# Long filters of a decoder layer: filter taps arranged by channel on GpSimd before TensorE reads them

## The reference, cut to what matters

```python
def fir(x, filt):                       # depthwise, causal, one filter per channel
    y = _dwconv_causal(x.reshape(b, Ll, H * DV), filt.reshape(H * DV, -1))
    return y.reshape(b, Ll, H, DV)
short, long_, wide = fir(v, fir_s), fir(v, fir_l), fir(v, fir_wd)   # 3, 31 and 64 taps
# the statistics of short, long_, wide, delta_out and v feed a gate, and
o = w_ctx[..., 0:1] * short + w_ctx[..., 1:2] * long_ + w_ctx[..., 2:3] * wide + w_ctx[..., 3:4] * delta_out + w_val * v
```

## Time and profile before

| | |
|---|---|
| three executions | 627.75, 627.02, 619.87 us; median 627.02 |
| the profiled execution | 627.85 us, of it span of the engines 626.1 us |
| mean granted TensorE clock | 0.956 of 2.4 GHz |
| HBM | 34.31 MB read, 2.10 MB written |

### The profile page before, as it was taken

The page is one execution under the profiler, slowest core; times in us unless marked ns, Lnnn a source line. Parts: engine busy times, 40 slices in busy tenths (PEclk is TensorE's granted clock), DMA queues, the critical chain, the costliest instruction groups (busy, mean ns, idle before and its releaser), DMA issues. The chain is left out here.

```text
span 626.1 us, 16517 instructions
## 1 busy us (share of the span) xinstructions
PE 540.1 (86%) x7254; PEld 409.9 (65%) x7254; DVE 444.3 (71%) x866; ACT 263.7 (42%) x478; POOL 117.5 (19%) x102
## 2 busy tenths in 40 slices
PE   4776879998999899988799889649999997998993
PEld 1454666767766766776564355538887876887883
DVE  1987758786787778785385999982445668768774
ACT  2675554452444245333237535322333243454441
POOL 1000550061006102601002220270810000010000
PEclk9899879999999999998799999788999998999997
DMA  6700630151014101312134100350000000000001
GB/s 191 237 3 0 199 107 3 37 170 37 4 56 156 33 4 58 115 36 84 56 136 136 34 17 18 113 181 33 1 1 0 2 1 1 0 2 35 9 25 68
DMA packets 26534, 37.47 MB, mean 60 GB/s; under 512 B 4641, under 2 KB 13602, under 8 KB 26463
## 3 DMA queue, kind: packets, MB, share of 16 engines
q1 hardware_dynamic: 26463, 36.42, 18.1%
HBM read 34.31 MB, written 2.10 MB: 58 GB/s over the span
## 5 line engine op out<-in xcount | busy, mean ns | idle before, releaser
L309 DVE SCALAR_TENSOR_TENSOR arena<-bank,conv_w,arena 128x511 f32<-128x511 f32 (+2 forms) x72 | 53.1, 746 | 17.5 <-ACT arena L468 14.2
L1534 POOL COPY arena<-v_win 128x256 f32<-128x256 f32 x32 | 20.3, 662 | 171.2 <-PE bank L786 171.1
L2068 ACT COPY arena<-bank 128x512 f32<-128x512 f32 x40 | 23.3, 585 | 56.4 <-PE bank L1818 37.3
L1818 PE MATMUL bank<-v_win,arena 128*128 128x256 f32 x192 | 46.1, 390 | 0.0
L1201 ACT COPY arena<-bank 128x512 f32<-128x512 f32 x40 | 21.7, 590 | 47.1 <-PE bank L912 47.0
L1818 PEld LDWEIGHTS bank<-v_win,arena 128*128 128x128 f32 x192 | 37.4, 196 | 5.7 <-issue 0.4
L786 PE MATMUL bank<-arena 128*32 128x128 f32 x512 | 35.7, 409 | 4.8 <-ACT arena L1151 3.1
L1800 PE MATMUL bank<-v_win,arena 128*128 128x256 f32 x128 | 32.2, 412 | 7.4 <-DVE arena L2353 4.3
L1156 ACT COPY arena<-bank 128x256 f32<-128x256 f32 x32 | 19.4, 606 | 44.5 <-PE bank L803 44.5
L1800 PEld LDWEIGHTS bank<-v_win,arena 128*128 128x128 f32 x128 | 26.5, 209 | 12.1 <-issue 4.5
L701 PE MATMUL bank<-arena 128*128 128x512 f32 x64 | 32.2, 624 | 0.9 <-PEq L704 0.9
(11 more groups left out here) (286 smaller groups left out, 1372.1 us busy)
## 6 DMA issues: line engine op xcount, KB each, us to landing
arena<-in_toep_w SPq DMA_DIRECT2D x32, 256.0 KB, 3.0
arena<-in_toep_l SPq DMA_DIRECT2D x32, 256.0 KB, 3.8
arena<-in_xT SPq DMA_DIRECT2D x12, 512.0 KB, 4.4
arena<-in_x SPq DMA_DIRECT2D x4, 512.0 KB, 4.2
arena<-in_ctx SPq DMA_DIRECT2D x4, 512.0 KB, 4.3
out<-arena SPq DMA_DIRECT2D x4, 512.0 KB, 2.9
qkv_w<-in_qkv_wT SPq DMA_DIRECT2D x1, 768.0 KB, 5.4
v_win<-in_w_gateT SPq DMA_DIRECT2D x1, 768.0 KB, 4.6
```

The source lines that it names most:

```text
L309: return nc.vector.scalar_tensor_tensor(out=acc[:, j:L], in0=src[:, 0:L - j], scalar=conv_w[:, m, CONV_K - 1 - j:CONV_K - j], in1=acc[:, j:L],
L1534: g.tensor_copy(A2["v_piece"][:, n % 2, :, :].rearrange("p c (t two) -> p t two c", two=2), v_win[:, :, :, n * PIECE:(n + 1) * PIECE].rear ...
L1818: i = mm(oo, src[:, k, f * P:(f + 1) * P], w[:, k, :], start=(k == 0), stop=(k == KT - 1 and f > 0))
L2068: nc.scalar.copy(dst(i), bank[RING_FIRST + n % RING].rearrange("p (t c) -> p t c", c=dst(i).shape[-1]))\
```

## The change

- **Arranging.** From piece 8 (`OPENING`) on, POOL copies each loaded piece from (f, c) to (c, f) order (`arrange`: 128 x 1024 words, read 8 words apart, written side by side), and the moving operand of L786 becomes 128 neighbouring words. `filter_piece(n)` waits for the new semaphore `arranged` instead of the DMA. Pieces 0 to 7 are moved as before.
- **Places.** `TOEP_BUFS` is 5: four places in the arena and one that takes the room of the three biases. The opening uses all five for raw pieces. Afterwards places 0 and 1 are raw, and 3, 4, 2 hold arranged pieces in turn; `arrange(n)` waits until piece n - 3 is done, the load of piece n until piece n - 2 is arranged.
- **POOL's order.** Three pieces are arranged before recurrence 0; then each `copy_piece(n)` is mostly followed by `arrange(n + 1)`, before and after `k_root` and behind `v_scale`.
- **SP's order.** The loads of raw pieces are gated by `arranged`, and the gate weights and the x of block 3 by the last two arrangements.
- **Biases.** Their loads leave block 1 and come in block 3, after a memset by POOL (768 words) at its start; two memsets leave block 1 (`PADS` 15 to 13).

```diff
-TOEP_BUFS = 4
+TOEP_BUFS = 5
+OPENING = 8
-PADS = 15
+PADS = 13
-        xq_b = sb("xq_b", [P, D])
-        xkv_b = sb("xkv_b", [P, 2 * D])
-        xo_b = sb("xo_b", [P, D])
+        late_rows = sb("late_rows", [P, 4 * D])
+        xq_b, xkv_b, xo_b = late_rows[:, 0:D], late_rows[:, D:3 * D], late_rows[:, 3 * D:4 * D]
...
+        raw_slot = lambda n: n % TOEP_BUFS if n < OPENING else n % 2
+        by_channel = lambda n: toep[(3, 4, 2)[(n - OPENING) % 3]].rearrange("p f c -> p (f c)").rearrange("p (c f) -> p c f", c=PIECE)
+        arranged_to = lambda n: n + 1 - OPENING
...
-                load(xq_b[0:1, :], dr["xq_b"].rearrange("(a n) -> a n", a=1))
-                load(xkv_b[0:1, :], dr["xkv_b"].rearrange("(a n) -> a n", a=1))
-                load(xo_b[:], dr["xo_b"].partition_broadcast(P))
...
+                def toep_from(first, last):
+                    for n in range(first, min(last, NPIECE - 1) + 1):
+                        if n < OPENING + 2:
+                            sp.wait_ge(s2["fir_mm"].sem, n - TOEP_BUFS + 1 if n < OPENING else n - 2)
+                        else:
+                            sp.wait_ge(s2["arranged"].sem, arranged_to(n - 2))
+                        load_toep(sp, n)
...
-                    pe.wait_ge(toep_in[n % TOEP_BUFS], 32 * (n // TOEP_BUFS + 1))
+                    if n < OPENING:
+                        pe.wait_ge(toep_in[raw_slot(n)], 32 * times_loaded(n))
+                        taps = toep[raw_slot(n)].rearrange("p f c -> p c f")
+                    else:
+                        pe.wait_ge(s2["arranged"].sem, arranged_to(n))
+                        taps = by_channel(n)
...
-                               A2["v_piece"][:, n % 2, c, :], toep[n % TOEP_BUFS][:, :, c], start=True, stop=True)
+                               A2["v_piece"][:, n % 2, c, :], taps[:, c, :], start=True, stop=True)
...
+                def arrange(n):
+                    pool.wait_ge(toep_in[raw_slot(n)], 32 * times_loaded(n))
+                    pool.wait_ge(s2["fir_mm"].sem, (4, 5, 8)[n - OPENING] if n < OPENING + 3 else n - 2)
+                    g.tensor_copy(by_channel(n), toep[raw_slot(n)].rearrange("p f c -> p c f")).then_inc(s2["arranged"].sem, 1)
...
+                arrange(OPENING)
                 copy_piece(OPENING)
+                arrange(OPENING + 1)
                 copy_piece(OPENING + 1)
+                arrange(OPENING + 2)
...
+                    copy_and_arrange(piece[2], piece[2])
+                    copy_piece(piece[3])
+                    k_root(b + 1)
+                    arrange(piece[4])
+                    copy_and_arrange(piece[4], piece[-1] - 1)
+                    copy_piece(piece[-1])
+                    q_roots(b + 1)
+                    v_scale(b + 1)
+                    arrange(piece[-1] + 1)
+                    copy_and_arrange(piece[-1] + 1, FIRST_OF[b + 1] + 1)
...
+                g.memset(late_rows[:, 0:3 * D], 0.0).then_inc(s4["sentinels"].sem, 1)
```

More of the change, by code:

```diff
@@ L265, in layer @@
         TOEP = 2 * DK * PIECE
-        toep = [arena[:, WL + i * TOEP:WL + (i + 1) * TOEP].rearrange("p (f c) -> p f c", c=PIECE) for i in range(TOEP_BUFS)]
+        toep = [arena[:, WL + i * TOEP:WL + (i + 1) * TOEP] for i in range(TOEP_BUFS - 1)] + [late_rows[:, :]]
+        toep = [x.rearrange("p (f c) -> p f c", c=PIECE) for x in toep]
         A2 = carve(arena, {
@@ L288, in load_keys_xT @@
             sp.dma_start(A2["xT"], dr["xT"][b].rearrange("(k p) t -> p k t", p=P)).then_inc(s2["xT_in"].sem, 16)
+        raw_slot = lambda n: n % TOEP_BUFS if n < OPENING else n % 2
+        times_loaded = lambda n: sum(raw_slot(k) == raw_slot(n) for k in range(n + 1))
+        by_channel = lambda n: toep[(3, 4, 2)[(n - OPENING) % 3]].rearrange("p f c -> p (f c)").rearrange("p (c f) -> p c f", c=PIECE)
+        arranged_to = lambda n: n + 1 - OPENING
         def load_toep(sp, piece):
-            i = piece % TOEP_BUFS
+            i = raw_slot(piece)
             for f in range(2):
@@ L706, in _ @@
             def _(sp):
[L708 to L715, removed]
+                def toep_from(first, last):
[5 more added lines that the diff above has]
+                        load_toep(sp, n)
+                toep_from(TOEP_BUFS, OPENING - 1)
                 sp.wait_ge(s2["beta_mm"].sem, 1)
                 load_keys_xT(sp, 1)
[L718 to L729, removed]
+                at = OPENING
+                for b in range(B - 2):
+                    toep_from(at, FIRST_OF[b] + 4)
+                    at = FIRST_OF[b] + 5
+                    sp.wait_ge(s2["beta_mm"].sem, s2["beta_mm"].at(b + 1, 1))
+                    load_keys_xT(sp, b + 2)
+                toep_from(at, NPIECE - 1)
+                sp.wait_ge(s2["arranged"].sem, arranged_to(NPIECE - 2))
                 sp.dma_start(g1x_w, dr["g1x_wT"].rearrange("(k p) n -> p k n", p=P)).then_inc(g1x_in.sem, 16)
-                sp.wait_ge(s2["fir_mm"].sem, NPIECE - TOEP_BUFS + 2)
+                sp.wait_ge(s2["arranged"].sem, arranged_to(NPIECE - 1))
                 load_turned_rows(sp, 0)
@@ L1566, in _, with copy_and_arrange @@
                 v_scale(0)
+                arrange(OPENING)
                 copy_piece(OPENING)
+                arrange(OPENING + 1)
                 copy_piece(OPENING + 1)
+                arrange(OPENING + 2)
+                def copy_and_arrange(first, last):
+                    for n in range(first, last + 1):
+                        copy_piece(n)
+                        if n + 1 < NPIECE:
+                            arrange(n + 1)
                 for b in range(B):
                     piece = pieces_of(b)
[L1571 to L1581, removed]
+                    if b == B - 1:
+                        copy_piece(piece[2])
+                        continue
+                    copy_and_arrange(piece[2], piece[2])
[8 more added lines that the diff above has]
+                    copy_and_arrange(piece[-1] + 1, FIRST_OF[b + 1] + 1)
         def of_batch(b):
@@ L1693, in _ @@
                 load_rows(sp, 1)
+                sp.wait_ge(s4["sentinels"].sem, 1)
+                sp.dma_start(xq_b[0:1, :], dr["xq_b"].rearrange("(a n) -> a n", a=1)).then_inc(dc_loaded.sem, 16)
+                sp.dma_start(xkv_b[0:1, :], dr["xkv_b"].rearrange("(a n) -> a n", a=1)).then_inc(dc_loaded.sem, 16)
+                sp.dma_start(xo_b, dr["xo_b"].partition_broadcast(P)).then_inc(dc_loaded.sem, 16)
                 for b in range(2, B):
```

15 lines of the change are left out of this document (7 added, 8 removed).

## The result

The changed kernel takes 620.22 us (median of 20 executions, 615.91 to 625.92), the kernel before, on the same chip, 625.64 us (median of 20, 618.35 to 629.49). The ratio is 0.9934 with a 95% interval of 0.9912 to 0.9957: 0.7% less, 0.4 to 0.9% by the interval, and so within 2% of no change. A ratio leaves out the slower executions of a kernel (over 1.5% above its fastest) and a median keeps them, so a ratio can differ from that of the medians: here the ratio means 4.1 us and the medians 5.4 us. The forecast of 629 us had the wrong sign.

A forecast was written before the change was run, and what follows sets the result against it. In the recurrences PE (busy 86%) and DVE were taken as two halves of a chain, DVE's waits limiting the gain. -0.8 + 1.75 + 1.75 + 1.3 - 2.2 = +1.8 us, 628.8 against the median, said as 629; range 617 to 637.

The forecast's parts named there:

- step 4: Recurrence 0: arrange(13), 135.3 to 137.7 us, holds L1338, which ends at 139.3 instead of 138.15: +0.6 us.
- step 6: End of recurrence 0: arrange(14) and arrange(15) fall on both L1354; the second ends at 152.6 instead of 150.85: +1.75 us.
- the signs named beforehand: Trace observations listed as showing the forecast right: L786 at 0.64 us, a POOL copy of 2.3 to 2.6 us, held DVE lines.
- The matmuls, 0.64 us: Pieces 8 to 31 on PE: 1.11 us falls to 0.64; undisturbed -1.2 us each in recurrences 0 and 1, -0.7 in 2.
- The rival of matmuls that do not get shorter: PE's pieces: four matmuls side by side, not the stride, make 1.11 us; gains vanish, holds stay: 634 us, chance 0.05.
- The arrangement, 2.4 us: POOL's strided copy of 1024 words, 24 times: 2.4 us each, with 0.97 and 2.6 us carried as ends.
- Step 1: Start of recurrence 0: arrange(11), 126.4 to 128.8 us, holds L1324, which ends at about 128.85 instead of 128.35: +0.5 us.
- Batch 3, -2.2: Pieces 25 to 31: 25 gains nothing, the others 0.47 or 0.27 us each; -2.2 us, bounds 0 and -3.3.
- Biases, -0.8: Block 1: bias loads leave the queue before batch 2's x, which comes 1.05 us earlier: -0.8 us, bounds -1.05 and 0.
- POOL late: Rival at piece 12: an arrangement of 2.8 us or more makes POOL late; at 4 us, 640 us in all; chance 0.09.
- Short holds: Rival: an arrangement near 1 us, or one that lets DVE through, gives -6.1 us, 621 us; chance 0.25.
- Clock and stalls: Rival: more PE idle time could bring the low clock into a recurrence, 4 us either way; chance 0.11, half each side.

The follow-up runs named there:

- the host's order: Kernel before with biases moved and the host laying out pieces by channel from piece 8, nothing arranged: 619.77 us, ratio 0.9871; run again 617.09 us, 0.9867.
- the two repeats: The changed kernel, unaltered, timed twice more beside later experiments against the kernel before: 619.51 us, ratio 0.9888, and 620.7 us, ratio 0.9852.
- arrangements behind the masks: Changed kernel, but POOL waits after v_scale until DVE has finished both L1357 before arranging the next recurrence's first piece: 620.28 us, ratio 0.992.

## Why the prediction was wrong

In short: the mechanism was right, and its price was too high. For recurrences 0 to 2 the forecast set 7.9 us of holds against 3.1 us of gain. Compared at like clocks the arrangements cost 3.6 us there, and the shorter matmuls give 4.1 to 4.5 us. The terms that failed are step 4, +0.6 us where about nothing was held, and step 6, 1.65 us where 0.55 was; both go back in part to the arrangement, taken at 2.4 us where it is 2.07. Of the signs named beforehand, PE's pieces at 0.64 us, the x of batch 2 earlier by 1 us or more, and no wait of PE for an arrangement came; a copy of 2.3 to 2.6 us, L1324 over 0.9, L1338 over 2 us for two and L1354 over 1.5 us did not.

**The matmuls, 0.64 us: right, its yield in the recurrences too low.** Recurrence 0 with neighbouring words and no arranging is 58.12 us in all three profiles, 1.57 us under before; I gave 1.2. In recurrence 2 it is 30.05 us, 1.1 us less; I gave 0.7. The limit "only what the small waits around DVE allow" was too tight by 0.4 us each. The rival of matmuls that do not get shorter is out.

**The arrangement, 2.4 us: too high, it is 2.07.** I took the value near the upper bound because its strides looked like those of `copy_piece`. This size decided more than itself, since steps 4 and 6 asked whether a copy runs into an instruction.

**Step 1, L1324 held: the hold is there, but it falls on L1317.** DVE, changed kernel:

```profile
122.34 1.21 DVE L1309 TENSOR_TENSOR arena<-arena 128x1024 f32<-128x1024 f32 x1
...
124.93 1.09 DVE L1320 TENSOR_SCALAR arena<-arena 128x16 f32<-128x16 f32 x1
125.94 0.66 DVE L1322 TENSOR_SCALAR arena<-arena 128x16 f32<-128x16 f32 x1
...
126.92 0.17 DVE L1327 TENSOR_TENSOR arena<-arena 128x16 f32<-128x16 f32 x1
```

and POOL beside it:

```profile
123.90 2.09 POOL L1544 COPY arena<-arena 128x1024 f32<-128x1024 f32 x1
125.91 0.66 POOL L1537 COPY arena<-v_win 128x256 f32<-128x256 f32 x1
```

L1320, 16 words with one input, ends at 126.02, with the arrangement (125.99); L1322 ends at 126.60, with the `copy_piece` behind it (126.57). The question that I had left open, whether L1317 and L1319 are held too, is answered: L1320 took 1.07 to 1.09 us in all nine recurrences of the three profiles of the changed kernel, L1322 0.66 us in three of the nine and 0.16 in the others. Recurrence 0 from piece 8 to the first L1357 takes 21.68 us in the profile shown, in the host's order 20.61: +1.07 us, against +0.5 in the sum, or +1.1 with the 0.6 us that I had set aside. In the two repeats, where L1322 was free, it is 21.14 and 21.15, so +0.5: the size of the sum, though by another instruction. My sentence that the two engines collide when both read two or more streams doesn't stand: L1320 and the copy read one each. The Trainium skill, SBUF — State Buffer, section Who interferes with whom, names `tensor_scalar` among the operations that, under conditions, can take the shared pair of ports. The trace agrees, and that sentence would have turned the open term into a counted one.

**Step 4, L1338 held: did not happen.** `arrange(13)` ended before it:

```profile
132.51 2.10 POOL L1544 COPY arena<-arena 128x1024 f32<-128x1024 f32 x1
134.53 0.68 POOL L1537 COPY arena<-v_win 128x256 f32<-128x256 f32 x1
135.04 5.47 POOL L1556 TENSOR_TENSOR arena<-arena,half_exp 128x32 f32<-128x32 f32 x1
```

Measured from the start of piece 8 (124.84 before, 122.50 after), I had it from 10.5 to 12.9 us; it ran from 10.0 to 12.1, and L1341 began at 12.6, with a `copy_piece` and then a power operation beside it. It took 1.36 us for its two halves, before 1.28. The +0.6 is about 0. The copy was over earlier than forecast (a shorter arrangement in front of it and a shorter one itself), and L1341, forecast at 12.1 us as before, came 0.5 us later since step 1 had cost more. The first of these is enough: in the two repeats `arrange(13)` ended at 11.6 us and L1341 began at 12.1.

**Step 6, both L1354 held, total delay +1.75 us, 1.65 of it here: the main failure, by size.** POOL and then DVE, changed kernel:

```profile
142.98 2.07 POOL L1544 COPY arena<-arena 128x1024 f32<-128x1024 f32 x1
144.99 1.10 POOL L1537 COPY arena<-v_win 128x256 f32<-128x256 f32 x1
145.95 2.06 POOL L1544 COPY late_rows<-arena 128x1024 f32<-128x1024 f32 x1
```

```profile
144.18 1.43 DVE L1357 TENSOR_TENSOR arena<-arena,c_ident 128x512 f32<-128x512 f32 x1
...
147.32 1.25 DVE L1357 TENSOR_TENSOR arena<-arena,c_ident 128x512 f32<-128x512 f32 x1
```

Both are held, but each begins more than half-way into a copy (1.20 and 1.37 us in), when 0.87 and 0.69 us of it are left. They take 0.74 and 0.56 us more than the 0.69 of the earlier trace rows, where I had 1.3 us each. From the first L1357 to piece 14 it takes 38.06 us, in the host's order and before 37.51: 0.55 us on the path. The rule by which I priced a hold was not the error, since step 6 too counted only what is left of the copy. The place of meeting was. I had the first L1354 begin 0.9 us into a copy of 2.4 us, with 1.5 us left, so that its hold outgrew the 0.80 us wait before L1455 and pushed the second L1354 0.44 us back, 1.0 us into the next copy. In the run the copy was 0.33 us shorter and L1357 met it 0.3 us later, so the first hold stayed inside that wait: the second L1357 starts 3.14 us behind the first, as before, and only its own 0.56 us reach the path. In all profiles with strided copies the growth of a held L1320 or L1357 is 0.13 to 0.14 us less than what was left when it started, with 0.68 to 1.77 us left. The `copy_piece` between them took 1.10 us instead of 0.65, its first half beside L1357: the hold works both ways.

**Recurrences together.** Recurrence 0 adds up: -1.57 (matmuls) + 1.07 + 0.55 = +0.05, and the two profiles' windows give +0.05; in the repeats it is -0.46 and -0.19. Over pieces 8 to 25 I forecast +4.8 us. The changed kernel has 152.0, 150.6 and 150.6, the kernels with strided reads and no arranging 151.1 and 151.5: on the mean -0.2, and -0.5 to -0.9 without the 152.0, whose clock in recurrence 1 was 0.97. This 5 us is the main part of the miss and turned its sign.

**Batch 3, -2.2: right in kind, and overlaid.** Granted clock and stalls of PE differ from execution to execution there; the stalls marked "issue" fall on the same instructions in every kernel. Before and then changed:

```profile
286.80 0.42 PE L897 MATMUL bank<-arena 64*64 64x32 f32 x12 [1.75 <-issue]
...
300.77 0.21 PE L939 MATMUL bank<-arena 64*64 64x64 f32 x1 [1.53 <-issue]
```

```profile
283.76 0.42 PE L900 MATMUL bank<-arena 64*64 64x32 f32 x12 [1.20 <-issue]
...
296.98 0.21 PE L942 MATMUL bank<-arena 64*64 64x64 f32 x1 [1.29 <-issue]
```

| pieces 25 to 31 | length | clock | issue stalls | length less stalls |
|---|---|---|---|---|
| before | 37.11 | 0.86 | 3.80 | 33.3 |
| biases alone | 35.77 | 0.90 | 3.09 | 32.7 |
| arranged, read strided | 34.14 | 0.90 | 1.84 | 32.3 |
| changed, second profile | 32.91 | 0.90 | 1.95 | 31.0 |
| changed, first and third | 32.28, 30.01 | 1.00 | 3.78, 1.76 | 28.5, 28.3 |
| host's order, second | 32.58 | 1.00 | 4.22 | 28.4 |

At a clock of 0.90, strided reads leave 32.3 and 32.7 us and neighbouring words 31.0: 1.3 to 1.7 us of gain, a little under the forecast. Two profiles not in the table point the same way: 31.7 us with neighbouring words at 0.85 (arrangements behind the masks), 33.3 with strided ones at 0.86 (before). At full clock, arranged or not, 28.3 to 28.5. The clock is worth about 2.5 us in this stretch. Whether shorter pieces make the full clock likelier isn't settled: it came in four of the ten profiles with neighbouring words and in none of the three with strided ones, which is too few.

**Biases, -0.8: likely, not shown.** The x of batch 2 lands at 18.15, 17.78 and 17.89 us in the changed kernel, 18.30 with the biases alone, and 20.18 before: 1.9 to 2.4 us earlier, where I gave 1.05. Piece 0 of the changed kernel starts at 62.56, 62.08 and 61.39 us, 1.2 to 2.4 us earlier than before (63.77), but with the biases alone at 63.72. The clock up to there differs too: 0.96, 0.99 and 0.99 against 0.96 before and 0.93 with the biases alone. At the clock of before, 0.96 to 0.97, five profiles of kernels with the biases moved have piece 0 at 62.41 to 62.94 us, 0.8 to 1.4 us earlier. That agrees with the forecast, but for before there is only one profile.

**The other rivals.** POOL late decided from 2.8 us for an arrangement; it takes 2.07 and PE never waited for one in the changed kernel. (The argument that nothing on POOL takes over 2.5 ns per word holds for copies and products only: `k_root` took 2.90 us for 16 words.) Short holds had the right sum, 621 us, by luck: an arrangement of 1 us indeed held L1320 not at all and gave the full gain, but the real one is 2.07 us and does hold, and the recurrences gave some 0.5 us where that rival had 3.1. Clock and stalls do more than the 4 us either way that I gave: the totals of the changed kernel span 612.7 to 625.9 us.

**The whole.** By the medians the change is worth 5.4 us in its own comparison, by the ratio 4.1. Without the shorter matmuls there is no gain to be seen: with all else equal and strided reads the ratio is 0.9985, with neighbouring words 0.9934, 0.9888 and 0.9852. In the profiles, pieces 8 to 25 take 150.6 to 152.0 us in the changed kernel and 156.8 with strided reads. By stretches compared at like clocks the change gives 0.5 to 0.9 us in the recurrences, 1.3 to 1.7 in batch 3 and perhaps 0.8 to 1.4 in block 1, so 2.6 to 4 us; the rest of what the totals show, more in the repeats, stays open, with the fifth place as the untested rival. The arrangements cost 3.6 us over pieces 8 to 25 at like clocks (150.6 against 147.0 of the host's order at full clock, 152.0 against 148.4 with recurrence 1 at 0.97), most of what the shorter matmuls give in that part, and the host's order, which pays nothing for it, is at 617 to 620 us no clearly better kernel: what is left of the difference is smaller than the spread of executions.

## What to carry to other kernels

A long GpSimd copy or product over SBUF can hold a VectorE instruction that reads SBUF, and then only for what is left of it when the other comes. So set its price by where the two meet, and check how that place moves when the copy is shorter or longer than you think: in step 6 a copy 0.33 us shorter, met 0.3 us later, cost 1.1 us less. Look for the growth of busy time at the same instruction count to see it. Count small one-input operations between two SBUF places among those that can be held. Judge a gain of 1% stretch by stretch against an experiment that has the gain without the price and one that has the price without the gain: a total can hide 5 us of cost behind clock and stalls.

## What the runs showed of the hardware

- L1320 and L1357 of VectorE, when they start under an arrangement or `v_scale` of GpSimd, grow by what is left of it less 0.14 us: L1320 (`tensor_scalar`, 128 x 16) by 0.92 us with 1.06 left, L1357 by 0.74 with 0.87 left, by 0.56 with 0.69 left, and under `v_scale` by 1.63 with 1.77 left. Not every GpSimd instruction holds in this way: under the power operation of `q_roots` with 4.70 us to go the second half of L1341, which has both inputs in SBUF, took 0.68 us, no more than elsewhere, and under a `copy_piece` with 0.58 us left L1341 grew by only 0.25 us.
- A GpSimd copy of 128 x 1024 fp32 words takes 1.04 us with neighbouring words and 2.07 us when it reads 8 words apart: twice as long. The Trainium skill, GPSIMD Engine Reference, Performance pitfalls for Q7 kernels, gives 2.9 cycles against 1.9 per element, from which I had estimated 2.5 us; here it would be 2.4 against 1.2 cycles at that page's 1.2 GHz. The page speaks of kernels written for the Q7 cores, and this is the built-in copy. The measurement decides: the step costs more than the page says, and both copies are faster.
- A TensorE piece whose moving operand is 8 words apart takes 1.11 us, with neighbouring words 0.64 us, in the same place, with the same windows as its stationary operand. So it was the stride and not the four matmuls side by side.
- PE stood still for "issue" at the first twelve matmuls of the same line (L897, L900 or its like) in every profile of every kernel, between 0.65 and 2.29 us, and at L939 or its like between 0.24 and 2.39 us. Its length varies by 1.6 us and more between executions of programs that are alike there, which is much of what one comparison of totals measures.
